# A GRU that feeds a mixture-of-experts FFN, one core: last unit in two halves, last product in fp32, earlier weight pieces, other first loads

## The reference, cut to what matters

```python
# x [32,32,256], cond [32,256]; D=256
def cell(h, xt):                       # 32 steps, one after the other
    gi = xt @ W_ih + b_ih; gh = h @ W_hh + b_hh
    r = sigmoid(i_r + h_r); z = sigmoid(i_z + h_z); n = tanh(i_n + r * h_n)
    return (1 - z) * n + z * h
hs = scan(cell, cond, x over time)     # [32,32,256] -> 1024 tokens
probs = softmax(hs @ w_router)         # 128 experts, top 4, weights renormalised
basis = silu(hs @ w_gate) * (hs @ w_up)            # 8 basis functions of 128
mixed = sum over experts and basis of (weight * scale * mix[expert, k]) * basis[k]
out = mixed @ w_down + (silu(hs @ sw_gate) * (hs @ sw_up)) @ sw_down
return x + out
```

## Time and profile before

| | us |
|---|---|
| median of 3 runs (lowest, highest) | 148.21 (148.15, 151.74) |
| the profiled execution's own time | 147.87 |
| its span, first to last instruction | 146.0 |
| PE busy | 136.3 (93%) |
| DVE busy | 111.6 (76%) |
| ACT, POOL busy | 68.1, 68.9 (47% each) |

### The profile page before, as it was taken

One profiled execution on the slowest core, in us unless ns is written; L12 is line 12 of the kernel. 1 busy time (PEld: TensorE's weight loads), 2 busy tenths in 40 slices (PEclk: granted clock), 3 DMA queues, 4 the chain that ended last, 5 costly groups with the idle time before them and its releaser, 6 DMA issues.

```text
span 146.0 us, 4048 instructions
## 1 busy us (share of the span) xinstructions
PE 136.3 (93%) x1494; PEld 98.0 (67%) x1494; DVE 111.6 (76%) x411; ACT 68.1 (47%) x222; POOL 68.9 (47%) x123
## 2 busy tenths in 40 slices
PE   7997999999679989999999999999999998899981
PEld 5565767766347658766876687668766875597881
DVE  2215588998967997898789878987898789949661
ACT  1204638565557345535553555255526541522830
POOL 2201115667754893466147614751475148566030
PEclk9999999999999999999999999999999999999999
DMA  3898970000000000010001000100010000000102
GB/s 97 270 369 288 343 235 5 7 0 2 0 0 4 0 0 4 4 36 4 0 0 40 0 0 0 43 0 0 7 36 0 4 7 31 0 0 0 36 4 72
DMA packets 5799, 7.12 MB, mean 49 GB/s; under 512 B 916, under 2 KB 4244, under 8 KB 5780
## 3 DMA queue, kind: packets, MB, share of 16 engines
q1 hardware_dynamic: 5472, 6.70, 13.7%
q10 hardware_dynamic: 308, 0.17, 0.4%
HBM read 5.81 MB, written 1.05 MB: 47 GB/s over the span
## 4 chain that ended last, share of the span: by engine, by line
PE 51%; DVE 34%; ACT 7%; issue 3%; POOL 1%; DVEq 0%
PE unit L604 18%; PE gates L595 11%; DVE sc_out L851 7%; PE down L674 6%; ACT sc_add L412 4%; DVE keys L934 4%; PE gates L559 4%; PE turned L744 3%; DVE pre L842 3%; DVE hT L858 3%; DVE m L839 2%; DVE p L899 2%; DVE wlo L871 2%; PE unit L574 2%; ACT trz L405 2%
## 5 line engine op out<-in xcount | busy, mean ns | idle before, releaser
L299 POOL CAST hThi<-hT 128x64 fp32r<-128x64 f32 x32 | 11.1, 347 | 54.5 <-DVE hT L858 54.1
L604 PE MATMUL unit<-whi,hThi 128*128 128x512 f32 x80 | 33.7, 421 | 2.7 <-POOL wlo L334 2.0
L604 PE MATMUL unit<-wlo,hThi 128*128 128x512 f32 x80 | 31.6, 395 | 0.0
L604 PE MATMUL unit<-whi,hTlo 128*128 128x512 f32 x80 | 31.6, 394 | 0.0
L405 ACT ACTIVATE trz<-gates 128x128 f32<-128x128 f32 x32 | 8.9, 277 | 43.8 <-PE gates L595 43.8
L595 PE MATMUL gates<-whh,hT 128*32 128x192 f32 x512 | 27.4, 332 | 1.7 <-DVE hT L858 1.1
L595 PEld LDWEIGHTS gates<-whh,hT 128*32 128x32 f32 x512 | 13.5, 109 | 12.7 <-DVE hT L858 5.6
L851 DVE TENSOR_TENSOR_SCAN sc_out<-sc_mul,sc_add 128x128 f32<-128x128 f32 x32 | 15.3, 479 | 8.0 <-ACT sc_add L412 7.7
L604 PEld LDWEIGHTS unit<-whi,hThi 128*128 128x128 f32 x80 | 15.1, 188 | 8.7 <-issue 3.5
L604 PEld LDWEIGHTS unit<-whi,hTlo 128*128 128x128 f32 x80 | 15.0, 188 | 3.5
L412 ACT ACTIVATE sc_add<-pre 128x64 f32<-128x64 f32 x32 | 10.3, 322 | 14.5 <-DVE pre L842 14.5
(11 more groups left out here) (129 smaller groups left out, 243.3 us busy)
## 6 DMA issues: line engine op xcount, KB each, us to landing
wraw<-in_L_ffn_w_gate_dram SPq DMA_DIRECT2D x2, 512.0 KB, 6.0
wraw<-in_L_ffn_w_up_dram SPq DMA_DIRECT2D x2, 512.0 KB, 7.8
out_dram<-ot SPq DMA_DIRECT2D x8, 128.0 KB, 2.0
xtok<-in_x_dram SPq DMA_DIRECT2D x7, 128.0 KB, 4.1
wih<-in_L_cond_W_ih_dram SPq DMA_DIRECT2D x2, 384.0 KB, 4.3
whh<-in_L_cond_W_hh_dram SPq DMA_DIRECT2D x1, 512.0 KB, 6.5
whh<-in_L_cond_W_hh_dram SPq DMA_DIRECT2D x1, 256.0 KB, 5.8
wraw<-L_ffn_shared_w_gate_dram SPq DMA_DIRECT2D x1, 256.0 KB, 7.5
```

What stands on the lines that cost most here:

```text
L299: pool.tensor_copy(hThi[:, c % 3, :, :, k], hT[:, c % 2, :, k, :]).then_inc(hThi_ready, 1)
L604: last = pe.matmul(dst, st[:, p % 3, s, :, :].rearrange("p b t -> p (b t)"), w[:, s, :, cols], start=(s == 0 and n == 0), stop=(s == KB - ...
```

## The change

- `WARM` goes from 16 to 10.
- `h0` is loaded by four DMAs of 32 rows each in place of one; DVE waits for all four.
- Chunks 2 and 3 of x are turned in step 0 in place of step 1, and ACT copies them there.
- All hi and lo pieces move one step forward.
- The three products of a block come as hi by hi, lo state by hi weight, hi state by lo weight; in chunk 0 only the third waits for the lo piece, the first for the hi piece.
- Unit 39 is made as two halves of 128 gate and 128 up columns, in banks 39 % 3 = 0 and 40 % 3 = 1; ACT, DVE and `last_mixed_turned` follow half by half.
- The last product is one fp32 matmul: DVE copies `last_turned` to `last_mixed`, PE multiplies it by the unsplit `draw[:, 0, :]`. The last `hi_turned` on ACT and `lo_turned` on DVE go.

```diff
-WARM = 16
+WARM = 10
-TURN_PAIR = {1: 2, 2: 4, 3: 6}
-KEEP_PAIR_SCALAR = {1: 2}
+TURN_PAIR = {0: 2, 2: 4, 3: 6}
+KEEP_PAIR_SCALAR = {0: 2}
-HI_AT = [(0, 0), (0, 0), (0, 0), (0, 2), (2, 4), (4, 6), (6, 8), (8, 10)]
-LO_VECTOR_AT = [[], [], [], [], [2], [4], [5], [8]]
-LO_POOL_AT = [[], [], [], [0], [1], [3], [6], [7], [9]]
+HI_AT = [(0, 0), (0, 0), (0, 2), (2, 4), (4, 6), (6, 8), (8, 10)]
+LO_VECTOR_AT = [[], [], [], [2], [4], [5], [8]]
+LO_POOL_AT = [[], [], [0], [1], [3], [6], [7], [9]]
...
-            act.dma_start(h0[:, :], cond.rearrange("b (j c) -> j b c", j=NJ)).then_inc(ld_h0, 16)
+            for j in range(NJ):
+                act.dma_start(h0[Q * j:Q * (j + 1), :], cond[:, FJ * j:FJ * (j + 1)]).then_inc(ld_h0, 16)
...
+            def last_half(k):                                  # ACT
+                n = NU * NC - 1
+                bank = unit_bank[(n + k) % NB]
+                cols = slice(I * k, I * (k + 1))
+                act.wait_ge(unit_ready, n + k + 1)
+                act.wait_ge(q_ready, n - 1)
+                act.activation(scaled_up[:, 1, cols], bank[:, I:2 * I], ACT.Copy,
+                               scale=coef[:, LAST % 2, K - 2 + k:K - 1 + k]).then_inc(up_scaled, 1)
+                act.activation(th[:, n % 2, cols], bank[:, 0:I], ACT.Tanh, scale=0.5).then_inc(th_ready, 1)
...
-                    for n, (st, w) in enumerate(((hThi, whi), (hThi, wlo), (hTlo, whi))):
+                    if p == 0:
+                        pe.wait_ge(w_hi, PIECES.index((u, s)) + 2)
+                    for n, (st, w) in enumerate(((hThi, whi), (hTlo, whi), (hThi, wlo))):
+                        if p == 0 and n == 2:
+                            wait_low(u, s)
...
+            def last_half(k):                                  # PE
+                n = NU * NC - 1
+                cols = slice(I * (K - 2 + k), I * (K - 1 + k))
+                pe.wait_ge(q_ready, n + k - NB + 1)
+                dst = unit_bank[(n + k) % NB][:, 0:2 * I].rearrange("p (g n) -> p g n", g=2)
+                for s in range(KB):
+                    for i, (st, w) in enumerate(((hThi, whi), (hTlo, whi), (hThi, wlo))):
+                        last = pe.matmul(dst, ..., w[:, s, :, cols], ...)
+                last.then_inc(unit_ready, 1)
...
-                pe.wait_ge(dhi_ready, LAST + 2)
-                for n, (st, w) in enumerate(((dhi, dhi_w), (dhi, dlo_w), (dlo, dhi_w))):
...
+                pe.wait_ge(last_mixed_ready, 1)
+                last = pe.matmul(last_down[:, 0:D], last_mixed[:, :], draw[:, 0, :],
+                                 start=False, stop=True, skip_group_check=True)
...
+            def last_half(k):                                  # DVE
+                n = NU * NC - 1
+                cols = slice(I * k, I * (k + 1))
+                dve.wait_ge(th_ready, n + k + 1)
+                dve.wait_ge(q_ready, n - 1)
+                dve.scalar_tensor_tensor(out=p1[:, n % 2, cols], ...)
+                dve.wait_ge(up_scaled, NU - 1 + k)
+                dve.tensor_tensor(q[:, LAST % 2, I * (K - 2 + k):I * (K - 1 + k)], ...)
+
+            def keep_last_mixed():
+                dve.wait_ge(turned_ready, LAST + 2)
+                dve.tensor_copy(last_mixed[:, :], last_turned[:, 0:P]).then_inc(last_mixed_ready, 1)
```

More of the change, by code:

```diff
@@ L138, in build @@
         dlo = sb("dlo", [P, 2, 3, P], F32R)
+        last_mixed = sb("last_mixed", [P, P])
         ot = sb("ot", [P, 2, D])
@@ L513, in _ @@
             copy_emT(LAST)
-            for u in range(NU - 1):
+            for u in range(NU - 2):
                 scale_up(u)
@@ L520, in _ @@
                     hi_turned(LAST - 1, turned, slice(0, 3), LAST + 1)
-            hi_turned(LAST, last_turned, slice(0, 1), LAST + 2)
+            last_half(0)
+            last_half(1)
         @block.tensor
@@ L598, in h_part, with wait_low, three @@
                 last.then_inc(gates_ready, 1)
-            def three(dst, p, cols, blocks):
-                for s in blocks:
-                    for n, (st, w) in enumerate(((hThi, whi), (hThi, wlo), (hTlo, whi))):
+            def wait_low(u, s):
+                i = PIECES.index((u, s))
+                if i in LO_VECTOR:
+                    pe.wait_ge(w_lo, LO_VECTOR.index(i) + 2)
+                else:
+                    pe.wait_ge(w_lo_pool, LO_POOL.index(i) + 1)
+            def three(dst, p, u, blocks):
+                cols = slice(UW * u, UW * (u + 1))
+                for s in blocks:
+                    if p == 0:
[3 more added lines that the diff above has]
+                            wait_low(u, s)
                         last = pe.matmul(dst, st[:, p % 3, s, :, :].rearrange("p b t -> p (b t)"), w[:, s, :, cols],
@@ L639, in unit @@
                         pe.wait_ge(early_ready, 1 + max(i for i in range(NE // 2) if i % len(early_bank) == n))
-                last = three(unit_bank[n % NB][:, :].rearrange("p (g n) -> p g n", g=2), p,
-                             slice(UW * u, UW * (u + 1)), blocks)
+                last = three(unit_bank[n % NB][:, :].rearrange("p (g n) -> p g n", g=2), p, u, blocks)
                 if KB - 1 in blocks:
                     last.then_inc(unit_ready, 1)
+            def last_half(k):
[5 more added lines that the diff above has]
+                    for i, (st, w) in enumerate(((hThi, whi), (hTlo, whi), (hThi, wlo))):
+                        last = pe.matmul(dst, st[:, LAST % 3, s, :, :].rearrange("p b t -> p (b t)"), w[:, s, :, cols],
+                                         start=(s == 0 and i == 0), stop=(s == KB - 1 and i == 2))
+                last.then_inc(unit_ready, 1)
             def turn_em(p):
@@ L784, in _ @@
             unit(n + 3, range(KB))
-            unit(n + 4, range(KB))
+            last_half(0)
+            last_half(1)
             last_shared_projected()
@@ L920, in scaled_q @@
                                   ALU.mult).then_inc(q_ready, 1)
+            def last_half(k):
[3 more added lines that the diff above has]
+                dve.wait_ge(q_ready, n - 1)
+                dve.scalar_tensor_tensor(out=p1[:, n % 2, cols], in0=th[:, n % 2, cols], scalar=1.0,
+                                         in1=unit_bank[(n + k) % NB][:, 0:I], op0=ALU.add, op1=ALU.mult)\
+                    .then_inc(p1_ready, 1)
+                dve.wait_ge(p1_ready, n + k + 1)
+                dve.wait_ge(up_scaled, NU - 1 + k)
+                dve.tensor_tensor(q[:, LAST % 2, I * (K - 2 + k):I * (K - 1 + k)], p1[:, n % 2, cols],
+                                  scaled_up[:, 1, cols], ALU.mult).then_inc(q_ready, 1)
+            def keep_last_mixed():
+                dve.wait_ge(turned_ready, LAST + 2)
+                dve.tensor_copy(last_mixed[:, :], last_turned[:, 0:P]).then_inc(last_mixed_ready, 1)
             def copy_logits(p):
@@ L1066, in _ @@
                     lo_turned(LAST - 1, turned, slice(0, 3), LAST + 1)
+            last_half(0)
+            last_half(1)
             residual(LAST - 1, down)
-            lo_turned(LAST, last_turned, slice(0, 1), LAST + 2)
+            keep_last_mixed()
             residual(LAST, last_down)
```

18 lines of the change are left out of this document (4 added, 14 removed).

## The result

| | before | after |
|---|---|---|
| median of all 16 runs, us | 148.44 | 149.75 |
| the profiled execution's own time | 147.87 | 148.78 |
| its span | 146.0 | 147.0 |
| ratio to before, 95% interval | | 1.0098, 1.0074 to 1.0121 |

By the ratio the change makes the kernel 1% slower; the forecast was 147.5 and a gain. One thing is needed to read this and what follows: TensorE's clock rises early in some runs of a kernel and late in others, some 3.6 us apart in time, and while every median here is of all runs, every ratio leaves out the runs that lie over 1.5% above the fastest of their kernel, which are seven of the 16 of the kernel before (151.6 to 152.2) and of the changed kernel only a stray of 329 us, since its other runs lie between, at 148.6 to 150.5.

The account below looks back on a forecast made before the run. PE, busy 93% of the span, was taken as the question in each stage. Start +0.1, steps 0 to 9 -1.06 and tail +0.22 summed to -0.74, forecasting 147.5 us by the runs' measure, range 145.9 to 149.5.

Parts of the forecast that it names:

- start: Up to `h_part(0)`: start moves from 10.07 to 10.18 us, +0.1, between -0.33 and +1.7.
- step 1 (turn in step 0): GRU step 1: PE has 0.98 us less to do, the chain takes over at 2.93, -0.48.
- step 4 (DVE's piece): GRU step 4: a piece on DVE now stands ahead of `m`, +0.85, bounds 0.44 and 0.88.
- steps 2 and 3 (DVE and POOL together): DVE and POOL meeting in step 2 (router remainder, part of `sc_add`): +0.10, bounds 0 to 0.3.
- step 8: GRU step 8: `em` can start at 37.02, not 38.00, and DVE's work up to `m` follows; -0.98, other bound -0.5.
- step 9: GRU step 9: unit 4 no longer waits 1.06 for POOL's low piece; -0.55, other bound -0.3.
- halves: Tail, unit 39: second half waits for DVE's `q` of unit 37; +0.25, bounds 0 and +0.4.
- last product: Tail, from last turn's end: DVE copy and one fp32 product take 1.05 against 1.08; -0.03, bounds -0.3 and +0.2.
- fewer warm-ups: -0.62: Start: PE begins the biases at about 4.02 instead of 4.64, -0.62 as far as chunk 1 of x.
- a rival at 0.10: Start: TensorE's clock stays low behind fewer warm-ups; start +2.1, whole kernel +1.3, 149.5 us; chance 0.10.
- h0 in four: Start, ACT's queue: four issues cost 1.8, chunk 1 goes out 1.1 late at 3.46 and lands at 7.76.
- The rival's landing of 9.4: Start: chunk 1 of x lands late at 9.4; start +1.7, whole kernel +0.9, 149.1 us; chance 0.12.

Follow-up runs that it names:

- experiment 2: Changed kernel with h0 loaded in one DMA again, WARM still 10; median 149.32 us, ratio to the kernel before 0.9977.
- Experiment 6: Kernel before with WARM 10 in place of 16, nothing else; median 151.0 us, ratio to the kernel before 1.018.
- the third experiment: Changed kernel with WARM 16 and h0 in one DMA again; median 146.96 us, ratio to the kernel before 0.9915.
- the fourth: Changed kernel with WARM 16, h0 in one DMA and unit 39 whole again; median 149.88 us, ratio to the kernel before 0.9909.
- the first experiment: Changed kernel with WARM 16 again, h0 still in four DMAs; median 150.41 us, ratio to the kernel before 1.0132.
- experiment 13: Changed kernel with WARM 20 and nothing else; median 148.09 us, ratio to the kernel before 0.9994.
- experiment 5: Kernel before with h0 in four DMAs, nothing else; median 150.71 us, ratio to the kernel before 1.0108.
- experiment 7: Changed kernel with WARM 16 and chunk 1 of x issued ahead of the four h0 DMAs; median 148.72 us, ratio to the kernel before 0.9911.
- the ninth: Changed kernel with WARM 24, h0 in one, unit 39 whole, without the 13 warm-ups between turns of x; median 148.11 us, ratio to before 0.9948.
- experiment 14: Kernel before with pieces one step forward, chunks 2 and 3 turned in step 0, and WARM 20; median 147.31 us, ratio to before 0.9934.

## Why the prediction was wrong

The steps of the sum, with what was measured:

| term | forecast | measured |
|---|---|---|
| start | +0.1 | +2.29 |
| step 1 (turn in step 0) | -0.48 | -0.48 |
| step 4 (DVE's piece) | +0.85 | +0.56 |
| steps 2 and 3 (DVE and POOL together) | +0.10 | 0 |
| step 8 | -0.98 | -1.19 |
| step 9 | -0.55 | -0.53 |
| other steps to 11 | 0 | +0.05 |
| halves | +0.25 | +0.27 |
| last product | -0.03 | +0.03 at most |

**The start is the step that failed**, and within it "fewer warm-ups: -0.62". I took the work behind the warm-ups at its old durations. The prediction's own rows held the warning: 16 warm-ups at 0.215 each against 0.118 in the tail showed that the clock rose just as they ended, so that with six fewer PE could come to the small matmuls at 1.2 GHz. It did: from 4.09 to 9.58 the same work took 5.49 where it had taken 3.08 (4.64 to 7.72). I priced this as a rival at 0.10 with +2.1 for the start, near the +2.3 that the profile shows. By the rows before the change it deserved more: none of them had PE at the small matmuls at the low clock. That it was not certain either, experiment 2 shows, where the clock rose there. Experiment 6 puts the price of this edit alone at 3.4 of start in its profiled execution. The Trainium skill ("TensorE: Matmul & The Clock Gate", section on the HAM clock gate) states that the number of matmuls at the low clock varies from run to run of one kernel. The traces agree: with the same code up to `h_part(0)`, the first eight bias matmuls take 0.63 in the third experiment and 1.08 in the fourth. The prediction quoted it as an aside; it bore on the kernel before as well as on the change.

**h0 in four.** The issue was sized rightly: 1.82 for four, taken at 1.8, and chunk 1 went out at 3.49, forecast 3.46. What failed is the flight, taken at the median of 4.3 and measured as 6.24 in the changed kernel and 5.0, 5.2 and 5.6 in three others with four DMAs ahead (experiments 1, 13 and 5); a landing of 9.73 came where 7.76 was forecast. The median came mostly from the six loads that SP issues later, behind `whh`, and my upper end of 5.0 was too low. The rival's landing of 9.4 was near. The rule on the number of engines in the Trainium skill ("DMA: Bandwidth & Descriptors", section on why a DMA increments its semaphore by 16), from which the prediction argued for a shorter flight of chunk 1, may hold for `h0`, and no run here shows it. The flight of chunk 1 was not shorter: 5.0 to 6.24 with `h0` in four, 4.8 to 5.1 with `h0` in one ahead of it. Chunk 1 now goes out after both issues of `whh` (2.54 and 3.19) instead of before them, which would lengthen its flight; experiment 7 fits, as it puts it ahead and finds no wait, but no run separated that from the four DMAs in front.

**Two rivals came true together.** They were given 0.12 and 0.10 as if they excluded each other. In the profile of the changed kernel PE's slow work ended at 9.58 and the load at 9.73, so each hides most of the other's cost. How much each is worth there the medians can't say (with 16 warm-ups 150.41, with h0 in one 149.32, with both 146.96, with both and the unit whole 149.88), because late clocks come with 10 and with 16 warm-ups. The lowest runs are 148.64 for the changed kernel and 148.74 with 16 warm-ups, 146.59 with h0 in one, 146.78 and 146.36 with both. These point to the load as what holds the changed kernel back where the clock is early, but they are single runs, and no profile of them was kept.

**The middle.** The mechanism was right in each step. Step 8 had a bound of -0.98, "since `em` can't come before DVE is free", and gained 1.19. `em` began 0.25 behind `hT(7)` in place of 1.27, which is 1.02, and from `em` to `m` it was 1.52 in place of 1.69. The profile after:

```profile
39.39 0.28 DVE L991 SCALAR_TENSOR_TENSOR em<-marked,ex 128x128 f32<-128x128 f32 x1
```

0.28 against 0.48 before, when POOL subtracted beside it (the state's rest from 37.96, a piece from 38.28). Step 4 cost 0.56 and not 0.85: the piece took its 1.00, `m` came 2.24 behind `hT(3)` in place of 1.53 (+0.71, where I had 0.88), and from `m` to `hT(4)` 0.15 was given back, since the scan no longer waited for a slow `sc_add` of DVE as long.

**The tail** came as worked out: the loss of 0.26 ahead of the second half, and 1.08 from the last turn, the same as before, against 1.05 forecast.

## What to carry to other kernels

When warm-up work is cut, look at the spacing of equal matmuls at its end, not at the granted clock: if the last ones still run at the low rate, what stands behind them can run at it too, and for far longer than the time saved (to about 13 us here, for 0.6 saved). Judge such a change by the spread of many runs, because one profile shows one way that the clock took. A small load added to a queue costs its issue time and moves every later load of that queue behind whatever other queues have sent meanwhile; what a waiting engine needs first should be issued first. And two limits that lie side by side must be undone together, in runs with the same clock, before either is judged.

## What the runs showed of the hardware

- Before its first rise the clock is not in the records: the granted clock reads 1.00 from 1 us on while equal matmuls take 0.215 us per 256 columns, against 0.118 later. Only the durations tell the state there. A later fall is recorded: 0.50 from 7.2 to 10.6 in the second experiment, from 9.3 to 12.7 in the ninth.
- With 10 warm-ups on the kernel before the clock stayed low until about 13; with 10 and h0 in one it was up at 3.9, in the changed kernel at about 10. With 16 it was up between 4.0 and 5.1 in five profiles and low until about 13.7 in two. With 20 and 24, all six profiles had it up ahead of or during the bias matmuls, and of the 48 runs that keep the warm-ups between the turns one (150.78 in experiment 14) lies where late clocks lie, and one (149.54 in experiment 13) has a mean granted clock of 0.988, like the runs with a fall. The three longest of the changed kernel itself, at 150.2 to 150.54, have 0.973 or 0.974; no profile shows where. That PE is at work is not enough: in the first experiment it had work nearly all the time from 1.05 to 13 and ran at the 1.2 GHz level to about 13.7, with the small matmuls of the biases in between.
- Once up, the clock fell again behind a wait of 0.52 (second experiment) and of 0.62 us (the ninth), each at the start of the kernel, while a wait of 1.59 (experiment 5) did it no harm at much the same place, nor did the idle of PE's loads of 1.15 ahead of `h_part(1)`. So the length of the wait doesn't decide it; what does, no run here shows.
- DVE operations with all operands outside PSUM run longer while POOL subtracts: in the changed kernel a piece took 1.00 to 1.13 us beside a subtraction and 0.69 beside POOL's rounding of the state, and `em` took 0.48 beside one (the kernel before) and 0.28 without. The `m` and `pre` of the same steps, which read PSUM, stayed at 0.21 to 0.22.
